# Two cross attentions that follow their projections inside one block

## What is computed

```
q_hk = (hidden_q @ Wq.T).reshape(b, s, H, K)
q_big = einsum('bshk,hkq->bshq', q_hk, w_kc_q)
kv_rope = kv_c * cos + rotate_half(kv_c) * sin
q_r = einsum('bshq,hqr->bhsr', q_big, W_qr)
k_r = einsum('bld,hdr->bhlr', kv_rope, W_kr)
attn = softmax(einsum('bhsr,bhlr->bhsl', q_r, k_r))
ctx_c = einsum('bhsl,bld->bhsd', attn, kv_rope)
ctx_lat = einsum('bhsd,hkd->bshk', ctx_c, w_kc_kv)
out = ctx_lat.reshape(b, s, H * K) @ Wo.T
```

## Time and profile before

| | us |
|---|---|
| median of three runs | 779.67 |
| lowest, highest | 778.89, 780.49 |
| the profiled execution, its own time | 774.19 |
| its span, first to last instruction | 772.4 |
| last projection matmul of layer 0 ends | 69.5 |
| first score of layer 0 | 72.53 |
| last projection matmul of layer 1 ends | 410.6 |
| first score of layer 1 | 415.10 |

### The profile page before, as it was taken

The page is one execution under the profiler, slowest core; times in us unless marked ns, Lnnn a source line. Parts: engine busy times, 40 slices in busy tenths (PEclk is TensorE's granted clock), DMA queues, the critical chain, the costliest instruction groups (busy, mean ns, idle before and its releaser), DMA issues. The chain is left out here.

```text
span 772.4 us, 15774 instructions
## 1 busy us (share of the span) xinstructions
PE 685.5 (89%) x5490; PEld 462.7 (60%) x5490; DVE 584.1 (76%) x1149; ACT 418.9 (54%) x1317; POOL 384.8 (50%) x338
## 2 busy tenths in 40 slices
PE   5997899998767489999995999889999999999987
PEld 4664677687424354445333677567777776767754
DVE  4466789765788765757684899897888888889787
ACT  2565778654358422222335878255555656566575
POOL 1503555473146324434485555356576687777512
PEclk9998899998579589999998999999999999999999
DMA  6465000000110041710010000023331221211001
GB/s 195 132 188 220 1 3 1 1 2 1 59 38 1 0 140 38 239 54 1 1 41 1 2 2 2 1 62 98 117 111 46 62 62 44 62 43 42 2 0 57
DMA packets 33576, 41.97 MB, mean 54 GB/s; under 512 B 15073, under 2 KB 23265, under 8 KB 32609
## 3 DMA queue, kind: packets, MB, share of 16 engines
q1 hardware_dynamic: 33504, 41.06, 17.4%
HBM read 40.00 MB, written 1.05 MB: 53 GB/s over the span
## 5 line engine op out<-in xcount | busy, mean ns | idle before, releaser
L2140 POOL TENSOR_TENSOR ra_direct<-ra_direct,ra_crossed 128x512 f32<-128x512 f32 x64 | 81.2, 1270 | 73.6 <-DVE ra_crossed L2326 73.5
L717 ACT ACTIVATE c_probs<-bank,c_neg_max 128x128 f32<-128x128 f32 x256 | 91.2, 382 | 29.4 <-DVE c_neg_max L800 29.4
L2326 DVE SCALAR_TENSOR_TENSOR ra_crossed<-bank,ra_bias,ra_sin 64x512 f32<-64x512 f32 x128 | 96.0, 750 | 1.9
L753 POOL TENSOR_TENSOR c_probs<-c_probs,c_inverse 128x512 f32<-128x512 f32 x64 | 66.6, 1041 | 61.1 <-DVE c_inverse L771 61.1
L1553 POOL TENSOR_TENSOR r_turned<-r_times_a,r_times_b 128x1024 f32<-128x1024 f32 x24 | 56.4, 2351 | 70.6 <-DVE r_times_b L1769 70.6
L2275 ACT ACTIVATE ra_probs_t<-bank 64x256 f32<-64x256 f32 x64 | 24.2, 378 | 60.4 <-PE bank L2214 60.1
L717 ACT ACTIVATION_READ_ACCUMULATOR c_probs<-bank,c_neg_max 128x1 f32 x256 | 56.5, 221 | 0.0
L2283 ACT ACTIVATE ra_probs<-ra_masked,ra_neg_max 128x64 f32<-128x64 f32 x128 | 42.9, 336 | 20.0 <-DVE ra_neg_max L2346 19.7
L1850 POOL TENSOR_TENSOR ra_w_lo<-ra_raw,ra_w_hi 128x768 f16<-128x768 f32 x32 | 52.7, 1647 | 0.0
L58 PE MATMUL bank<-xt_hi,ra_w_hi 128*128 128x512 f16 x128 | 49.1, 384 | 0.9 <-PEq L599 0.9
L58 PE MATMUL bank<-xt_hi,ra_w_lo 128*128 128x512 f16 x128 | 49.0, 383 | 0.0
(11 more groups left out here) (271 smaller groups left out, 2082.0 us busy)
## 6 DMA issues: line engine op xcount, KB each, us to landing
ra_raw<-l_attn_w_dram SPq DMA_DIRECT2D x32, 384.0 KB, 3.0
wq<-l_wq_dram SPq DMA_DIRECT2D x16, 256.0 KB, 2.8
wo<-l_wo_dram SPq DMA_DIRECT2D x16, 256.0 KB, 3.4
wkcq<-l_wkcq_dram SPq DMA_DIRECT2D x16, 192.0 KB, 2.8
ra_wo<-l_attn_wo_dram SPq DMA_DIRECT2D x1, 2048.0 KB, 10.7
wqr<-l_wqr_dram SPq DMA_DIRECT2D x16, 96.0 KB, 2.3
wkv<-l_wkv_dram SPq DMA_DIRECT2D x16, 64.0 KB, 2.8
x_res<-x_dram SPq DMA_DIRECT2D x2, 512.0 KB, 5.6
```

The source lines that it names most:

```text
L717: e = nc.scalar.activation(probs[u][:, n, :], score_bank[u][q][:, n - q * HP, :], ACT.Exp, bias=neg_max[u][:, n:n + 1], accum_out=total[u] ...
L753: nc.gpsimd.tensor_tensor(out=probs[u][:, at, :], in0=probs[u][:, at, :], in1=inverse[u][:, at].unsqueeze(2).broadcast_to([P, HP, L]), op= ...
L2140: nc.gpsimd.tensor_tensor(out=direct[e][k][:], in0=direct[e][k][:], in1=crossed[k][:], op=ALU.add).then_inc(roped, 1)
L2326: ins = nc.vector.scalar_tensor_tensor(dst[out_lo:out_lo + rows].rearrange("p t (b s) -> p (t b) s", b=2), src[lo:lo + rows], bias[e][lo:l ...
```

## The change

The two blocks of a layer's cross attention become one. `cross_attention` turns into `cross_attention_steps`, which opens no block and returns the pieces (`score`, `exponentials`, `peak`, which is the two maxima of a batch, and the rest by engine); the projections call them at the end of their own lists. Nothing is computed otherwise.

- **Layer 0.** PE scores behind its last `project`; the first score waits until the low parts of half 0 are written (`lat.lo_done` at 30), score 8 and the first output product until all are. On DVE the maxima of batch 0 stand ahead of the last `lat.low`.
- **Layer 1.** PE scores batch 0 ahead of `fold(22)` and batch 1 ahead of `fold(23)`; ACT takes the exponentials of batch 0 ahead of the last four `high`; DVE takes the maxima of batch 0 right behind its last `rotate`, and the last `low` stand behind the maxima of batch 1 (first two) and of batch 2 (last two). The score banks are now (3, 4) and (0, 1), the others 2, 5, 6 and 7.
- **Weights.** `prep.split` of layer 0 is cut in three (one of 128x1536, two of 128x768) and stands on POOL behind the normalisations of batches 3, 4 and 5; the last `split_output_low` of layer 1 stands behind those of batch 1.
- **Memory.** Tiles of the attention share room with ones the projection is done with: `ctx_lo` with the raw keys in layer 0, most of them with `times_a`, `times_b` and `turned` in layer 1.

```diff
-    def split(pool):
-        pool.wait_ge(loaded, 16)
-        nc.gpsimd.tensor_scalar(m.attn_w_hi[:], raw[:], 1.0, 0.0, ALU.mult, ALU.add).then_inc(stepped, 1)
-        pool.wait_ge(stepped, 1)
-        nc.gpsimd.tensor_tensor(out=m.attn_w_lo[:], in0=raw[:], in1=m.attn_w_hi[:],
-                                op=ALU.subtract).then_inc(stepped, 1)
+    def split(pool, piece):
+        if piece == 0:
+            pool.wait_ge(loaded, 16)
+            nc.gpsimd.tensor_scalar(m.attn_w_hi[:], raw[:], 1.0, 0.0, ALU.mult, ALU.add).then_inc(stepped, 1)
+        else:
+            c = piece - 1
+            pool.wait_ge(stepped, 1)
+            nc.gpsimd.tensor_tensor(out=m.attn_w_lo[:, c, :], in0=raw[:, c, :], in1=m.attn_w_hi[:, c, :],
+                                    op=ALU.subtract).then_inc(stepped, 1)
...
+        att = cross_attention_steps(nc, g, own, "c0", ((0, 1), (6, 7), (2, 3), 4, 5),
+                                    (lat.lo_done, 4 * PAIRS - 2, 4 * PAIRS), room, weights)
...
-            prep.split(pool)
+
+            def between(j):
+                if 3 <= j < 6:
+                    prep.split(pool, j - 3)
+
+            att.gpsimd(pool, between)
...
             pair_loop(step)
+            att.tensor(pe)
...
             pair_loop(step)
+            att.scalar(act)
...
+                if n == PAIRS - 1:
+                    att.peak(dve, 0)
                 lat.low(dve, n, u, 1)
...
+    def score(pe, j):
+        u = j % 2
+        if j in (0, BH):
+            pe.wait_ge(queries, first_ready if j == 0 else all_ready)
+        for q in range(2):
+            wait(pe, exped, 2 * j + q - 3)
...
+            if b == 0 and begun:
+                pe.wait_ge(queries, all_ready - 2)
...
+                if t == 0:
+                    pe.wait_ge(queries, all_ready)
...
+        att = cross_attention_steps(nc, g, own, "c1", ((3, 4), (0, 1), (2, 5), 6, 7), (q_lo, 4 * (UNITS - 1), 4 * UNITS),
+                                    room)
...
-                elif at >= 2:
+                elif 2 <= at < PER_QUAD - 1:
                     split_output_low(nc, g, pool, at - 2)
+
+            def between(j):
+                if j == 1:
+                    split_output_low(nc, g, pool, 3)
+
+            att.gpsimd(pool, between)
...
-            for k in (STEPS - 2, STEPS - 1):
+            for j, k in enumerate((STEPS - 2, STEPS - 1)):
+                if j == 1:
+
+                    pe.wait_ge(multiplied, 2 * STEPS - 1)
+                att.score(pe, j)
                 fold(k)
+            pe.wait_ge(multiplied, 2 * STEPS)
+            att.tensor(pe, 2)
...
+            for q in range(2):
+                att.exponentials(act, 0, q)
             for side in range(2):
                 high(UNITS - 1, side)
+            att.scalar(act, 1)
...
-            for side in range(2):
-                low(UNITS - 1, side)
+            att.peak(dve, 0)
+
+            def between(j):
+                if j in (1, 2):
+                    low(UNITS - 1, j - 1)
+
+            att.vector(dve, 1, between)
```

More of the change, by code:

```diff
@@ L355, in ternary_weight_steps, with cross_project_plain @@
     return prep
-def cross_project_plain(nc, g):
+def cross_project_plain(nc, g, weights):
     m, a = g.m, g.a
@@ L831, in self_attention_cam @@
+    att = Fields()
+    att.score, att.exponentials, att.peak, att.ln = score, exponentials, peak, ln
+    att.tensor, att.scalar, att.gpsimd, att.vector = tensor, scalar, gpsimd, vector
+    return att
 def self_attention_cam(nc, g, ln, inputs, prep):
```

435 lines of the change are left out of this document (225 added, 210 removed).

## The result

The changed kernel takes 768.39 us (median of four runs, 766.55 to 770.74); the kernel before, run beside it, 779.28. The ratio is 0.986, with a 95% interval of 0.983 to 0.990, or 10.9 us less (8 to 13). The prediction was 770.0, with a range of 767.3 to 773.4. The profiled execution after took 766.55, with a span of 764.7, against 774.19 and 772.4.

A forecast was written before the change was run, and what follows sets the result against it. The attention was taken as bound by the loop maximum, exponentials, inversion, next maximum, so a head start of its first batches is kept. Layer 0's 2.73 plus layer 1's 7.0, 9.7 us, off 779.67 gives 770.0, range 767.3 to 773.4.

The forecast's parts named there:

- First score of layer 0: Start of layer 0's attention: PE's first score waits only for half 0's low parts, near 69.8, 2.73 us earlier.
- a first score after 72: Layer 0: an absolute time set down as a sign that the forecast is wrong; 69.8 was expected.
- Lead of layer 0: Layer 0's attention: the earlier first score is kept as a gain of 2.73 us, bounds 2.1 and 2.8.
- the loop does not go through the late inversion: Layer 0, batch 0: first inversion on DVE is 0.6 us late, but batch 1's maxima do not wait for it.
- Folds of layer 1: Layer 1's start: PE scores batches 0 and 1 within its 2.40 us wait for POOL's last sum, delaying no fold.
- ACT and DVE in layer 1: Layer 1's start: exponentials of batch 1 7.45 us earlier, maxima of batch 3 7.1; gain taken as 7.0, bounds 6.0 and 7.45.
- The give-back of 0.4: Layer 1, batches 2 to 3: the last low parts on DVE cost 0.36 us of the lead.
- POOL's pieces: Weight splits on POOL between batches: each delays a normalisation by at most 0.45 us, covered by 1.54 of slack; costed at nothing.
- Rival A: Layer 0's start: PE's clock holds at 2.4 GHz, gaining 0.79 us more, total 769.2; chance 0.15.
- Rival B: Layer 1's start: PE at half clock for the first batches, some 2.5 us lost, total 772.5; chance 0.18.
- Rival C: Attention: clock does not recover, each batch loses 4.2 us, slower than before at 783; chance 0.03.
- The sum: Whole kernel: 2.73 for layer 0 plus 7.0 for layer 1, 9.7 us off the median, giving 770.0.

The follow-up runs named there:

- e2: Only layer 1 merged, layer 0 put back to its two blocks, against the changed kernel; ratio 0.987 to the kernel before, 9.8 us less.
- e3: One block per layer but lists in the old order, against the changed kernel, so only the barrier goes; ratio 0.996 to the kernel before.
- e11: Against e10b: layer 1's last two low parts on DVE set apart, behind the maxima of batches 2 and 3; ratio 0.981 to the kernel before.
- e5: The changed kernel with all POOL weight splits back in front of the attentions; ratio 0.983 to the kernel before.
- e10b: Against e8: two of layer 1's last four high parts moved behind the exponentials of batch 1, low parts moved too; one execution, time not read.
- e12: e10b unaltered, timed: ratio 0.983 to the kernel before, 13.4 us less.
- e1: Only layer 0 merged, layer 1 put back to its two blocks, against the changed kernel; ratio 0.991 to the kernel before, 7.0 us less.
- e10: Against e8: exponentials of batches 0 and 1 both ahead of layer 1's last high parts, low parts later; one execution, time not read.
- e6: The changed kernel with layer 1's last four low parts together behind the maxima of batch 1; one execution, time not read.
- e8: The changed kernel with layer 1's third output-weight split on POOL moved behind batch 1, the fourth behind batch 2; ratio 0.985 to the kernel before.
- e7: The changed kernel with unread matmuls filling PE's gaps, 12 in layer 0 and 9 in layer 1; ratio 0.986 to the kernel before.

## Why the prediction was right, and where its steps were off

- **First score of layer 0.** Predicted 2.73 earlier, 0.04 behind the anchor; 2.71 earlier. The absolute sign set down for it, a first score after 72, did come (72.18), but by the later start of the whole projection; from the anchor the step held. The exponentials of batch 0 start 1.44 behind the anchor (predicted 1.40), the last low parts end at 3.45 (3.54), the first inversion is at 3.47.
- **Lead of layer 0.** 2.73 predicted, bounds 2.1 and 2.8; 2.6 measured against e2 and e3. The step "the loop does not go through the late inversion" held but for 0.1: the maxima of batch 1 come 3.87 behind those of batch 0, and 3.77 in e2. The barrier, taken at 0.33, is 0.27 in layer 0 and 0.23 in layer 1.
- **Folds of layer 1.** The scores went into PE's wait for POOL: last fold 3.04 behind the last product, before and after, with 1.17 of that wait left. Batch 0 took 0.9 as thought.
- **ACT and DVE in layer 1.** Exponentials of batch 1: 7.45 predicted, 7.47 measured. Maxima of batch 3: 7.1 predicted, 7.03 measured. The give-back of 0.4 by the low parts is 4.70 against 4.23 between batches 2 and 3, as worked out. e11, though on another order, shows that 0.2 of such a distance goes away with the low parts apart; that they are all of the 0.47 in the changed kernel was not shown. One reading was wrong: the prediction says that the lower clock cost nothing at layer 1's start in the trace before. It cost about 0.4 at the first scores, and since the forecast starts from that trace's 420.60, this part of the gain came into the 7.45 unseen.
- **POOL's pieces.** Called harmless, at most 0.45 late: the normalisation behind the second piece starts at 96.07, 0.44 later than it would behind its inversion, and DVE's period stays 4.22. e5 confirms it.
- **Rival A, the mis-sized term.** Its condition came true in part: of eleven traces with layer 0 merged, the clock held at its start in five (one of them filled), and in the others it was low for about 3 us. Its price of 0.79 was wrong as it was used. It is what one execution of the kernel before lost, with half clock for 10 us up to its first mix; e2 and e3, in the same old order and with 6 to 7 us of it, don't lose it, and in the merged layer 0 it was lost neither where the clock held nor where it fell. So it belongs to the baseline, not to whether the clock holds after the change. How many of the timed executions of before had this stall is not known.
- **Rival B, likewise.** Its mechanism is real: in all eight traces in which layer 1 starts by the changed order or one near it (all merged ones but e10b, e11 and e12), there was half clock at the start. But in the changed order it costs nothing or 0.6 to 0.8, where I took 2.5: one batch is late, not two. The forecast for layer 1 was 7.0; at batch 15 it is 6.2 to 7.1.
- **Rival C.** Half clock never reached the output products: in no trace does its stretch at the start of an attention last beyond 13.6 behind the anchor in layer 0 or 19 in layer 1, and in the changed kernel the products begin at 19.5 and 22.1. The chances given don't fit together here: C, slower than before, has 0.03, and "slower" has 0.02.
- **The sum.** 9.7 forecast; the leads in the traces make 2.6 and 6.2 to 7.1, so 9 to 10; the medians say 10.9 (8 to 13). They agree, but whether more than the leads is gained is open, as are the surpluses of e1 and e3. The steps of the sum held; that the median came within 1.6 of the forecast is in part luck, since what differs outside the seams is more than that: the anchor of layer 0 stood anywhere from 69.8 to 84.4, and the stretch between the layers at 307 or at 310 to 312. Each is as large as the effect of a seam, and both go in good part with how long PE's clock was at its lower level.

## What to carry to other kernels

Taking out a barrier is worth the barrier, 0.2 to 0.3 here; the gain comes from what may then be put in another order, above all the first links of the next loop under the last, waiting links of the one before. Cost it by the chain of one batch (maximum, exponentials, inversion) from an anchor that both traces share, since executions differ outside by half of the gain and more. And take a stall for a price only when a second trace shows it.

## What the runs showed of the hardware

- Half clock costs 0 to 0.8 by where it falls. In the old order of layer 1 it cost 0.4 at the first scores (first exponential 1.77 behind the first score, against 1.36), and then nothing: in e1 ten microseconds of it (9 to 19 behind the last product) left the distances as they are in before and e3 with some seven, and it was over just as the first mix ran (1.33 at 18.25). In layer 0 of the trace before it was not over then (mix 1.97), and 0.8 was lost. In the changed order, 3 us at 15 to 19 cost 0.6 to 0.8, because there DVE waits for the transposes, and 3 us at 10 to 13 cost nothing. In e10 it came ahead of the first mix, and between it and the late mix the whole lead of 2.6 was gone by batch 3.
- The fall goes with PE's gaps in part, but no gap of these traces decides it alone. In layer 0 ten merged traces have the same gap of 2.8 ahead of the first transposes; six were at half clock for about 3 us behind it and four never. In layer 1, with the longest gaps ahead of the first mix, 3.66 and 3.79 (e6, e10), the clock was low for about 7 us; with 2.8 to 2.95 (the changed kernel twice, e2, e8) for about 3. In e10b, e11 and e12, with gaps of 1.94 and less, it never fell there; in e5 and e7, with nothing over 1.94 ahead of the fall either, it did. And in e12 and e3 its mean was 0.53 over 18 us in which the trace has PE busy throughout. "TensorE: Matmul & The Clock Gate" of the Trainium skill (Part 1) says that activity releases the throttle, and that how many matmuls run slow differs from run to run. The second agrees: in the two traces of the changed kernel the slow ones are the first mix in one (1.97) and the second mix and the transposes behind it in the other (1.88 and 1.93). The first does not explain the 18 us of e12 and e3.
- The table load ahead of layer 1's exponentials (1.28 at 401.36) lay in ACT's idle time and delayed nothing: the first exponential stands 0.71 behind its maxima, as others do.
